# Attention softmax of a four-layer transformer kernel: hand-over between engines per half of the query rows

## The reference

```python
q = (text_hidden @ Wq).reshape(B, T_text, N_HEADS, HEAD_DIM).transpose(0, 2, 1, 3)
k = (vision_tokens @ Wk).reshape(B, T_vis, N_KV_HEADS, HEAD_DIM).transpose(0, 2, 1, 3)
v = (vision_tokens @ Wv).reshape(B, T_vis, N_KV_HEADS, HEAD_DIM).transpose(0, 2, 1, 3)
...
scores = jnp.einsum('bhtd,bhsd->bhts', q, k) / scale
...
attn = jax.nn.softmax(scores, axis=-1)
...
out = jnp.einsum('bhts,bhsd->bhtd', attn, v)
...
return out @ Wo
```

## Time and profile before

| what | value |
|---|---|
| median of 3 runs | 419.43 us (418.96 to 420.85) |
| the profiled execution | 418.34 us |
| its span, first to last instruction | 416.5 us |
| PE busy | 398.7 us, 96% |
| PEld busy | 384.5 us, 92% |
| DVE busy | 300.3 us, 72% |
| ACT busy | 229.7 us, 55% |
| POOL busy | 163.7 us, 39% |
| granted TensorE clock | 1.000 over the span |

### The profile page before, as it was taken

One profiled execution on the slowest core, in us unless ns is written; L12 is line 12 of the kernel. 1 busy time (PEld: TensorE's weight loads), 2 busy tenths in 40 slices (PEclk: granted clock), 3 DMA queues, 4 the chain that ended last, 5 costly groups with the idle time before them and its releaser, 6 DMA issues.

```text
span 416.5 us, 8853 instructions
## 1 busy us (share of the span) xinstructions
PE 398.7 (96%) x3238; PEld 384.5 (92%) x3238; DVE 300.3 (72%) x942; ACT 229.7 (55%) x636; POOL 163.7 (39%) x261
## 2 busy tenths in 40 slices
PE   8898999999999999999999999999899999999896
PEld 7788899999889999999999999999899989999795
DVE  4788678879766879678667878777757766665644
ACT  1886876656643466566543456566553565655232
POOL 2012764754634233434443334245343233334231
PEclk9999999999999999999999999999999999999999
DMA  7999200000000200000000100000000000000000
GB/s 234 327 343 357 80 0 2 2 2 2 3 0 2 57 23 2 2 0 2 3 25 2 55 0 2 2 2 0 2 27 0 2 2 2 2 2 0 27 2 25
DMA packets 15098, 16.89 MB, mean 41 GB/s; under 512 B 1552, under 2 KB 14032, under 8 KB 15056
## 3 DMA queue, kind: packets, MB, share of 16 engines
q1 hardware_dynamic: 15056, 16.33, 12.2%
HBM read 15.28 MB, written 1.05 MB: 39 GB/s over the span
## 4 chain that ended last, share of the span: by engine, by line
PE 53%; DVE 22%; ACT 12%; POOL 5%; issue 4%; DMA 2%; SPq 1%; DVEq 0%; POOLq 0%
PE bank_s L364 8%; PE bank_qa L364 7%; ACT prob L901 6%; DVE prob L1528 6%; PE bank_pt L364 4%; PE bank_s L554 3%; PE bank_pt L572 3%; PE bank_o L599 3%; PE bank_u L585 3%; DVE pt_lo L1539 3%; DMA w_raw<-in_w3T 2%; DVE ut_lo L1545 2%; PE bank_u L663 2%; PE bank_x L364 2%; PE bank_s L562 2%
## 5 line engine op out<-in xcount | busy, mean ns | idle before, releaser
L1179 POOL TENSOR_SCALAR prob<-prob,row_inv,valid_b 128x256 f32<-128x256 f32 x128 | 70.3, 559 | 100.2 <-DVE row_inv L1535 100.2
L901 ACT ACTIVATE prob<-prob,row_min 128x256 f32<-128x256 f32 x128 | 64.2, 502 | 69.2 <-DVE row_min L1528 69.2
L1539 DVE TENSOR_TENSOR pt_lo<-bank_pt,pt_hi 128x512 fp32r<-128x512 f32 x64 | 44.0, 688 | 17.7 <-ACT pt_hi L861 17.4
L1545 DVE TENSOR_TENSOR ut_lo<-bank_u,ut_hi 128x256 fp32r<-128x256 f32 x64 | 26.9, 420 | 33.3 <-ACT ut_hi L861 32.8
L1528 DVE CUSTOM_DVE_ANT_0 prob<-bank_s,masked 128x256 f32<-128x256 f32 x128 | 48.7, 418 | 2.7 <-PE bank_s L562 1.4
L861 ACT ACTIVATE pt_hi<-bank_pt 128x512 fp32r<-128x512 f32 x64 | 37.5, 586 | 8.8 <-PE bank_pt L572 8.7
L1191 POOL TENSOR_TENSOR act_lo<-act_raw,act_hi 128x256 fp32r<-128x256 f32 x32 | 24.1, 754 | 45.9 <-ACT act_hi L966 45.8
L572 PE MATMUL bank_pt<-ident,prob 128*128 128x128 f32 x256 | 39.1, 275 | 2.0 <-POOL prob L1179 1.7
L364 PE MATMUL bank_qa<-xt_hi,a_hi 128*128 128x256 f32 x126 | 39.5, 314 | 0.1
L364 PE MATMUL bank_qa<-xt_lo,a_hi 128*128 128x256 f32 x126 | 35.2, 279 | 0.0
L599 PE MATMUL bank_o<-c_hi,ut_hi 128*128 128x256 f32 x128 | 34.2, 290 | 1.0 <-ACT ut_hi L861 1.0
(11 more groups left out here) (315 smaller groups left out, 1291.7 us busy)
## 6 DMA issues: line engine op xcount, KB each, us to landing
wq_raw<-in_wqT SPq DMA_DIRECT2D x4, 512.0 KB, 8.9
wo_raw<-in_wo SPq DMA_DIRECT2D x4, 512.0 KB, 8.7
w_raw<-in_w12T SPq DMA_DIRECT2D x2, 704.0 KB, 7.7
gate_raw<-in_gateT SPq DMA_DIRECT2D x2, 576.0 KB, 7.7
up_raw<-in_upT SPq DMA_DIRECT2D x2, 576.0 KB, 9.5
down_raw<-in_downT SPq DMA_DIRECT2D x2, 576.0 KB, 11.4
x<-in_x SPq DMA_DIRECT2D x4, 256.0 KB, 4.6
guT<-in_guT SPq DMA_DIRECT2D x4, 256.0 KB, 3.3
```

Of the source, the lines that this page charges most:

```text
L901: last = act.activation(row, row, ACT.Exp, scale=-1.0, bias=row_min[:, h % 2, t:t + 1], accum_out=row_sum[:, h % 2, t:t + 1])
L1179: last = pool.tensor_scalar(row, row, row_inv[:, h % 2, t:t + 1], valid_b[:, 0:1], ALU.mult, ALU.mult)
L1539: dve.tensor_tensor(pt_lo[:, :, :].rearrange("p s t -> p (s t)"), bank["pt"][:, :], f32(pt_hi[:, :, :].rearrange("p s t -> p (s t)")), ALU ...
L1545: dve.tensor_tensor(ut_lo[:, :], bank["u"][:, 0:T], f32(ut_hi[:, :]), ALU.subtract).then_inc(S["u_l"], 1)
```

## The change

Each of the four counts goes up once for each half instead of once for a head, and each consumer waits for a half at a time. The minimum of half 0 lets ACT begin that half's exponential; its sum lets DVE take that half's reciprocal, which is now two instructions of 128x1 with a wait ahead of each; POOL waits and scales per half, with a no-op in each; and PE transposes half 0's two tiles after waiting for half 0 alone. In `turn_probs` the wait for `t_l` now stands first. The waits for `s_min` at the score banks are scaled to the new counts and wait for the same moment as before. No arithmetic changes.

```diff
@@ scores
-                    pe.wait_ge(S["s_min"], H * b + h - 1)
+                    pe.wait_ge(S["s_min"], NT * (H * b + h - 1))
@@ turn_probs
-                pe.wait_ge(S["s_norm"], H * b + h + 1)
                 if h >= 1:
                     pe.wait_ge(S["t_l"], H * b + h)
                 for t in range(NT):
+                    pe.wait_ge(S["s_norm"], NT * (H * b + h) + t + 1)
                     for s in range(2):
@@ exps
-                act.wait_ge(S["s_min"], H * b + h + 1)
-                for t in range(NT):
+                for t in range(NT):
+                    act.wait_ge(S["s_min"], NT * (H * b + h) + t + 1)
                     row = prob[:, h % 2, t, :]
-                    last = act.activation(row, row, ACT.Exp, scale=-1.0, bias=row_min[:, h % 2, t:t + 1],
-                                          accum_out=row_sum[:, h % 2, t:t + 1])
+                    act.activation(row, row, ACT.Exp, scale=-1.0, bias=row_min[:, h % 2, t:t + 1],
+                                   accum_out=row_sum[:, h % 2, t:t + 1]).then_inc(S["s_exp"], 1)
                     if t == 0 and between is not None:
                         between()
-                last.then_inc(S["s_exp"], 1)
@@ normalise
-                pool.wait_ge(S["s_inv"], H * b + h + 1)
-                pool.nop(nofuse=True)
-                for t in range(NT):
+                for t in range(NT):
+                    pool.wait_ge(S["s_inv"], NT * (H * b + h) + t + 1)
+                    pool.nop(nofuse=True)
                     row = prob[:, h % 2, t, :]
-                    last = pool.tensor_scalar(row, row, row_inv[:, h % 2, t:t + 1], valid_b[:, 0:1],
-                                              ALU.mult, ALU.mult)
-                last.then_inc(S["s_norm"], 1)
+                    pool.tensor_scalar(row, row, row_inv[:, h % 2, t:t + 1], valid_b[:, 0:1],
+                                       ALU.mult, ALU.mult).then_inc(S["s_norm"], 1)
@@ row_minima
-                    last = dve.tensor_tensor_reduce(out=prob[:, h % 2, t, :], in0=src[:, t * T:(t + 1) * T],
...
-                last.then_inc(S["s_min"], 1)
+                    dve.tensor_tensor_reduce(out=prob[:, h % 2, t, :], in0=src[:, t * T:(t + 1) * T],
...
+                                             ).then_inc(S["s_min"], 1)
@@ row_inverses
-                dve.wait_ge(S["s_exp"], H * b + h + 1)
-                dve.reciprocal(row_inv[:, h % 2, :], row_sum[:, h % 2, :]).then_inc(S["s_inv"], 1)
+                for t in range(NT):
+                    dve.wait_ge(S["s_exp"], NT * (H * b + h) + t + 1)
+                    dve.reciprocal(row_inv[:, h % 2, t:t + 1], row_sum[:, h % 2, t:t + 1]).then_inc(S["s_inv"], 1)
```

More of the change, by code:

```diff
@@ L745, in beside @@
                     if not last and (h, part) == (15, 1):
-                        pe.wait_ge(S["s_min"], H * (b + 1))
+                        pe.wait_ge(S["s_min"], NT * H * (b + 1))
                         bit_up(b + 1, 0)
@@ L1527, in row_minima @@
                 for t in range(NT):
-                    last = dve.tensor_tensor_reduce(out=prob[:, h % 2, t, :], in0=src[:, t * T:(t + 1) * T],
-                                                    in1=masked[:, :], scale=1.0, scalar=3.0e38, op0=ALU.add,
-                                                    op1=ALU.min, accum_out=row_min[:, h % 2, t:t + 1])
-                last.then_inc(S["s_min"], 1)
+                    dve.tensor_tensor_reduce(out=prob[:, h % 2, t, :], in0=src[:, t * T:(t + 1) * T],
+                                             in1=masked[:, :], scale=1.0, scalar=3.0e38, op0=ALU.add,
+                                             op1=ALU.min, accum_out=row_min[:, h % 2, t:t + 1]
+                                             ).then_inc(S["s_min"], 1)
             def row_inverses(b, h):
-                dve.wait_ge(S["s_exp"], H * b + h + 1)
-                dve.reciprocal(row_inv[:, h % 2, :], row_sum[:, h % 2, :]).then_inc(S["s_inv"], 1)
+                for t in range(NT):
+                    dve.wait_ge(S["s_exp"], NT * (H * b + h) + t + 1)
+                    dve.reciprocal(row_inv[:, h % 2, t:t + 1], row_sum[:, h % 2, t:t + 1]).then_inc(S["s_inv"], 1)
             def probs_lo(b, h):
```

## The result

The changed kernel took **418.19 us**, median of 18 runs (414.62 to 419.12); the kernel before, run beside it, 420.30 (18 runs, 418.08 to 421.81). The ratio is 0.9943 [0.9923, 0.9963]: 0.57% faster, 2.1 us, where 3.2 us were forecast (416.2).

A forecast was written before the change was run, and what follows sets the result against it. PE's own work bounds plain heads, neck and neck with a DVE-ACT loop; only stalls can be gained. 1.32 + 0.62 + 0.46 + 0.48 + 0.30 + 0.27 - 0.21 = 3.24 us, so 419.43 - 3.2 = 416.2 us, range 414.0 to 419.7.

The forecast's parts named there:

- first rival: Batch ends: what PE gained earlier in batches 0 to 2 is waited away; gain 1.2 us, 418.2 us; chance 0.16.
- Losses: DVE-bound batch-end chains (batches 1, 2) and batch 0 between turns 11 and 12: 0.07 each, 0.21 us lost.
- Exponential one pitch earlier: DVE-ACT loop: ACT starts the first exponential after the first minimum, so the loop loses 0.34 us.
- Extra reciprocal 0.07: DVE: two reciprocals for one cost 0.07 us more per head, 4.5 us for 64, in DVE's idle time.
- drain rival: DVE: a reciprocal costs its whole 0.155 us, felt at fourteen DVE-bound places; gain 2.0, 417.4 us; chance 0.10.
- Turn by halves: PE turns behind POOL's rounding, heads 5 and 12, batches 0 to 2: two transposes hidden, 6 x 0.22 = 1.32 us.
- slower rival: PE: the second wait breaks the transposes in all 64 turns, 0.10 us each; 422.6 us; chance 0.07.
- First turn of batch 3: PE's stall of 0.70 us ahead of this turn shrinks, by as much as the loop carries on: 0.62 us gained.
- qa_lo at head 2: Query matmuls waiting for DVE's qa_lo lose 0.23 us; the shorter loop removes that in batches 1 and 2: 0.46.
- At head 8: Query matmuls waiting for qa_lo: 0.16 of 0.24 us gained each in batches 0 to 2, 0.48; batch 3 0.30.
- Batch 0's projection: The projection that waits for ut_hi at the end of batch 0 comes earlier: 0.27 us gained.
- the one from the trace to the median: Whole kernel: profiled 418.34 - 3.2 = 415.1 us; the median is 1.1 higher, so 419.43 - 3.2 = 416.2 us.

The follow-up runs named there:

- e9: Kernel before, with the router's matmuls mixed among wide ones in batches 0 to 2 and 18 unread transposes in the last layernorm wait: 418.65 us, ratio 0.9975.
- e8: Changed kernel, with the router's matmuls mixed among wide ones in batches 0 to 2 and 18 unread transposes in the last layernorm wait: 414.86 us, ratio 0.9882.
- e1: Kernel before, with only the minimum counted for each half and ACT waiting for a half at a time: 419.39 us, ratio 0.9976.
- e4: Kernel before, with only the reciprocal of both halves split into two of 128x1: 420.62 us, ratio 1.0021.
- e3: Changed kernel, but with one reciprocal of 128x2 and one count of the sums, as before: 418.52 us, ratio 0.9933.
- first group: Experiments ran beside the kernel before in two groups on two chips; before's median was 420.20 us (35 runs) in the first, 419.42 (23 runs) in the second.
- e6: Changed kernel, with unread transposes filling PE's pauses, 8 at each batch end and 18 in the last layernorm wait: 417.48 us, ratio 0.9925.
- e2: Kernel before, with only POOL's scaling counted for each half and the turn waiting for a half at a time: 418.55 us, ratio 0.9962.
- e7: Changed kernel, with the router's twelve small matmuls placed one after each matmul of wide chunk 1 in batches 0 to 2: 415.70 us, ratio 0.9897.

## Why the prediction was half right

The measured 418.19 us lies in the stated range, but not in the forecast's own part of it (415.0 to 417.3). It lies on the figure of the first rival, 418.2, whose mechanism did not happen (see *Losses*). So it was in part luck that the range held: it was drawn wide for rivals, and what moved the time was none of them.

**The change's own gain was forecast well: 3.2 us, and 3.4 to 4.0 measured.** In the profiled executions PE runs the same 3238 matmuls in the same order, so the start of each can be set against before. From a batch's first turn to its last, with the 0.62 by which batch 3's first turn comes earlier counted to that batch:

| batch | forecast, by its terms | from the traces |
|---|---|---|
| 0 | 0.44 + 0.16 + 0.27 - 0.07 = 0.80 | 0.71 |
| 1 | 0.44 + 0.23 + 0.16 - 0.07 = 0.76 | 0.82 |
| 2 | the same, 0.76 | 0.80 |
| 3 | 0.62 + 0.30 = 0.92 | 0.62 + 0.48 = 1.10 |
| sum | 3.24 | 3.43 |

The two figures without traces, 3.8 (e9 against e8) and 4.0 (after against before at full clock, an estimate), are a little higher; what lies outside these stretches isn't resolved.

Step by step:
- *Exponential one pitch earlier:* right (0.12 behind the first read). In e1 it carries 2.30 us turn to turn, about two thirds of the whole.
- *Extra reciprocal 0.07, and hidden:* right, by e4; nearly hidden by e3 (0.2 us turn to turn). The drain rival asked 0.15 for each and a gain of 2.0 in all. The Trainium skill (VectorE: DVE Perf Modes, "The DRAIN you can't avoid") has the next DVE operation wait for an empty pipe, and adds that one that is not held starts earlier. The prediction left the addition out; pt_lo starting 0.14 after the first of two reciprocals of 0.148 agrees with the addition and not with a wait in every case.
- *POOL by halves at nothing:* right (1.09 against 1.08).
- *Turn by halves, 0.22 each at heads 5 and 12:* right. Turn 5 moves by 0.22, 0.21 and 0.22; turn 12 starts 0.43 to 0.44 earlier, gives 0.23 of it back in its middle, and keeps 0.20 to 0.21. The slower rival (0.10 for each split turn) is refuted: the undisturbed turn at 157.66 takes 0.60 as in the earlier trace rows. Plain heads stayed at 3.28 to 3.30.
- *First turn of batch 3, 0.62:* the size was right, the place not. The turn starts 0.62 earlier, without a gap, but the loop behind it had not moved as far, and the first query now waits for qa_lo and gives 0.52 back; the gain appears at the projection, 0.55 earlier. PE there:

```profile
328.54 0.41 PE L671 MATMUL bank_o<-down_hi,act_lo 128*128 128x256 f32 x2
328.78 0.60 PE L572 MATMUL bank_pt<-ident,prob 128*128 128x128 f32 x4
329.66 0.38 PE L364 MATMUL bank_qa<-xt_hi,a_hi 128*128 128x256 f32 x1 [0.28 <-DVE qa_lo L1507]
```

- *qa_lo at head 2, 0.23 each:* right (0.24 and 0.23). *At head 8, 0.16 each in batches 0 to 2:* nearly right, 0.11 to 0.15 from the turn of head 8 to that of head 9 (0.14 to 0.25 in e1 and e3, which keep one reciprocal); in batch 3 0.29 against 0.30.
- *Batch 0's projection, 0.27:* it starts 0.27 earlier and gives that back at once, as L603 now waits for ut_lo; from turn 13 to turn 15, 0.13 is kept. Too large by half. The turn of head 11 there, which I had not counted, comes 0.26 earlier and loses it again before turn 12.
- *Losses, 3 x 0.07:* the size was right, the place not shown: after's stretches of batches 0 to 2 are 0.10, 0.04 and 0.08 us longer than those of e3, with one reciprocal. At the batch ends nothing shows. The wait for xt_lo there is 3.3 us before and after, and the gains ahead of it were kept (from the last turn of batches 0 and 1 to the next first turn nothing is lost beyond 0.01): the first rival is refuted as well.

**The step that failed is the one from the trace to the median.** It took 3.2 from the profiled execution and then added 1.1, since the median of the runs shown was 1.1 above it, as if that distance belonged to every execution alike. That distance is mostly the clock: before's runs at 0.999 or more have medians of 418.95 and 418.64, 0.5 to 0.8 of the 1.1 lower. The profiled execution of before ran at 1.000, its runs in the first group at 0.994 in the mean and in the second at 0.997; those of after at 0.992. On the scale of the profile, without falls, the forecast was 418.34 - 3.2 = 415.1, and after's three runs at clock 1.000 took 414.62, 414.69 and 415.36. By the estimate the falls of after take 0.0076 of 417 us, 3.2 us in the mean; those of before 2.4 us in the first group and 1.3 in the second. So 0.8 to 1.9 of the 4.0 us at full clock should be lost. In the means of the 18 and 18 runs (420.28 and 417.51) 2.8 us are left, and in the medians 2.1, as 12 of after's 18 runs had a clock of 0.992 or less. The clocks of these 18 runs of before are not known. No step of the forecast had a term for the clock.

**What stays open** is why after's executions fall more often. The router's row stands in both kernels, and the clock is higher with the edits in both (0.997 to 0.999 for before with the two, on one chip; 0.992 to 0.997 for after with the mixing alone, in two sets). The low clocks go with the earlier exponential: e1, e3, e6 and after lie at 0.991 to 0.994, and before, e2 and e4 at 0.994 to 0.997. That holds for seven kernels and may be chance; no run shows what links them. Nor is it shown that the 18 transposes take away the falls at the end of the last wait: of the profiles with them (e6, e8, e9) none has one there, but of the seven without only three do (after, e3, e7).

## What to carry to other kernels

A count for each half is worth its instructions where the consumer stalls on it, and only up to the next engine's bound: here the minimum's and the scaling's counts paid, the reciprocal's did not, and part of the turn's gain alone was waited away (e2). Before two profiles are compared, or a forecast is moved from a profile to a median, look at the granted clock of each execution: a difference of 1 to 2 us between runs of one kernel was one fall of 3.4 us. And set the starts of the same instructions side by side: here four profiles agree on the gain within 0.06 us, where whole times of after spread by 4. In this kernel a row of small matmuls on a full PE was at times followed by a fall that cost 1.5 us; spread among wide ones it was not.

## What the runs showed that was not expected

- A row of twelve matmuls of 8 columns, PE busy throughout, stands ahead of 8 clock falls in seven profiles; with one wide matmul between each two of them none of three profiles has a fall there, and e7 lies 1.9 to 2.5 us under after.
- PE's pauses at the batch ends and in the last wait, filled with transposes, made hardly a difference (0.9935 against 0.9924).
- Behind the transposes of a turn the first query takes 0.21 to its successor (158.01 to 158.22), the later ones 0.12; the wider pitch that the earlier trace rows shows behind a wait stands behind a turn without one, too. Why is not shown.
